# Angle and rope tables in two parts, early products of ones, and transpositions inside a unit's products

## The reference

```
w = weights[subjects]
x = x + einsum('bct,bcd->bdt', x, w)
```

```
q = rope(rmsnorm(x @ Wq.T, q_norm_w), pos)          # k likewise; v = x @ Wv.T
freqs = pos[..., None] * inv_freq                   # pos = cache_seqlens + arange(32)
rope(t) = concat([t1*cos - t2*sin, t2*cos + t1*sin])  # sin, cos of freqs
o = softmax(q @ k_all.T * SCALE, masked) @ v_all
x = x + o @ Wo.T
```

## Time and profile before

| | |
|---|---|
| median of three runs | 1021.69 us |
| lowest, highest | 1018.34, 1025.10 us |
| span of the profiled execution | 1018.6 us |
| TensorE busy | 965.9 us (95%) |
| VectorE, ScalarE, GpSimd busy | 821.1, 738.2, 536.8 us |
| first product of unit 0 | 20.44 us |
| first product of units 1, 2, 3 | 26.62, 31.51, 37.44 us |
| first product of unit 8 (chunk 1) | 64.31 us |

### The profile page before, as it was taken

The page is one execution under the profiler, slowest core; times in us unless marked ns, Lnnn a source line. Parts: engine busy times, 40 slices in busy tenths (PEclk is TensorE's granted clock), DMA queues, the critical chain, the costliest instruction groups (busy, mean ns, idle before and its releaser), DMA issues.

```text
span 1018.6 us, 24766 instructions
## 1 busy us (share of the span) xinstructions
PE 965.9 (95%) x8097; PEld 799.2 (78%) x8097; DVE 821.1 (81%) x1755; ACT 738.2 (72%) x2007; POOL 536.8 (53%) x706
## 2 busy tenths in 40 slices
PE   4889999999889988899999999999999999989998
PEld 2668888888677777787788888888888888878885
DVE  6779999999998688878877777877787787877770
ACT  4888999988784687877767676767676776767660
POOL 4445565655893057655555464455445544544440
PEclk9999999999999999999999999999999999999999
DMA  5789999989997979999999998999998999999950
GB/s 197 252 271 319 326 391 362 386 294 381 393 350 250 377 268 330 357 280 249 258 301 284 275 292 280 312 264 284 321 278 258 317 296 251 311 279 288 265 125 11
DMA packets 249903, 294.89 MB, mean 290 GB/s; under 512 B 79024, under 2 KB 206512, under 8 KB 247216
## 3 DMA queue, kind: packets, MB, share of 16 engines
q1 hardware_dynamic: 231088, 226.07, 74.6%
q0 software_dynamic: 18688, 67.25, 17.6%
HBM read 231.77 MB, written 46.27 MB: 273 GB/s over the span
## 4 chain that ended last, share of the span: by engine, by line
PE 69%; DVE 14%; issue 6%; ACT 5%; POOL 3%; DMA 1%; SPq 1%; DVEq 0%; ACTq 0%; POOLq 0%
PE ps_proj L1465 16%; PE ps_y L1465 15%; PE ps_o L1540 13%; PE ps_s L1503 7%; PE ps_t L1514 7%; PE ps_s L1507 6%; PE ps_rt L1611 2%; DVE c_stage L1361 2%; DVE rot L1333 2%; DVE probs L1209 2%; DVE stage L1347 1%; PE ps_t L1522 1%; PE ps_o L1552 1%; DVE rot L1325 1%; POOL probs L920 1%
## 5 line engine op out<-in xcount | busy, mean ns | idle before, releaser
L920 POOL TENSOR_SCALAR probs<-probs,recip 128x544 f32<-128x544 f32 (+1 forms) x256 | 162.4, 635 | 298.0 <-DVE recip L1217 290.8
L994 ACT ACTIVATE probs<-probs,neg_max 128x544 f32<-128x544 f32 x256 | 191.5, 748 | 148.9 <-DVE neg_max L1209 132.5
L1209 DVE CUSTOM_DVE_ANT_0 probs<-ps_s,mask,row_scale 128x544 f32<-128x544 f32 x256 | 200.4, 783 | 65.9 <-PE ps_s L1507 50.0
L1540 PE MATMUL ps_o<-pt,vs 128*128 128x128 f16 x3072 | 213.3, 219 | 0.5 <-DMA vs<-v_pages,v_row 0.5
L1540 PEld LDWEIGHTS ps_o<-pt,vs 128*128 128x128 f16 x3072 | 192.7, 98 | 14.9 <-DMA vs<-v_pages,v_row 0.9
L874 POOL TENSOR_TENSOR roped<-rot 128x256 f32<-128x256 f32 x160 | 144.2, 923 | 81.2 <-DVE rot L1325 78.1
L1229 DVE SCALAR_TENSOR_TENSOR pt<-ps_t,pt 128x512 f16<-128x512 f32 x190 | 130.0, 684 | 48.7 <-ACT pt L1000 42.7
L1465 PE MATMUL ps_proj<-wt_hi,x0t_hi 128*128 128x512 f32 x384 | 159.6, 416 | 7.4 <-DVE x0t_lo L1167 6.4
L1465 PE MATMUL ps_y<-wo,ot_hi 128*128 128x512 f16 x512 | 153.5, 381 | 2.6 <-DVE ot_lo L1241 2.6
L1465 PE MATMUL ps_proj<-wt_hi,x0t_lo 128*128 128x512 f32 x384 | 151.8, 395 | 0.0
L1465 PE MATMUL ps_proj<-wt_lo,x0t_hi 128*128 128x512 f32 x384 | 150.8, 393 | 0.0
(11 more groups left out here) (153 smaller groups left out, 1644.0 us busy)
## 6 DMA issues: line engine op xcount, KB each, us to landing
kt<-k_pages_t SPq DMA_DIRECT2D x512, 128.0 KB
c_nat<-in_L_cond_k_cache SPq DMA_DIRECT2D x32, 512.0 KB, 6.0
q_t<-stage SPq DMA_DIRECT2D x64, 256.0 KB, 6.8
c_nat<-in_L_cond_v_cache SPq DMA_DIRECT2D x32, 512.0 KB, 7.2
qt<-q_t SPq DMA_DIRECT2D x32, 512.0 KB
w_nat<-in_L_cond_Wq SPq DMA_DIRECT2D x8, 1024.0 KB, 8.7
k_pages_t<-c_stage SPq DMA_DIRECT2D x16, 512.0 KB, 5.8
c_nat<-in_L_cond_Wo SPq DMA_DIRECT2D x16, 512.0 KB, 7.5
```

The costliest lines, as they stand in the source:

```text
L920: pool.tensor_scalar(part, part, col(recip, i), 1.0, ALU.mult, ALU.mult).then_inc(p_norm, 1)
L994: act.activation(pr, pr, ACT.Exp, bias=col(neg_max, i), scale=-1.0, accum_out=col(row_sum, i)).then_inc(a_exp, 1)
L1209: dve.tensor_tensor_reduce(out=probs_of(i), in0=ps_s[:, score_cols(i):score_cols(i) + KEYS], in1=mask[(i // HK) % 2][:, mask_at(i):mask_at ...
L1540: ins = pe.matmul(ps_o[n % 2][:, jl * P:(jl + 1) * P], v[:, part, :], pt[pt_slot(i)][:, NCH * half + c, :], start=jl == 1 and c == 0 and k ...
```

## The change

On VectorE the angle work and the query tables are made for token tiles 0 and 1 ahead of the loop; the angles of tiles 2 to 7 follow ahead of the loop too, with tile 1's lower part amid them, and their tables inside unit 0. The work on the norm weights moves ahead of all of it. On ScalarE the sines are in two pairs accordingly, the second ahead of unit 0's squares, a sine of one column is taken at the start, and tile 0's higher part moves between the weights' higher parts. On VectorE the whole-table operations of lines 1267 to 1282, with the lower parts that followed them, are replaced by the calls shown; the seven operations on the norm weights are unchanged. On TensorE products of ones by ones, whose result nobody reads, stand at three places of the head, and in chunk 0 the transpositions of the next tile stand between the sixth and the seventh product. GpSimd issues three gathers instead of four ahead of the first weight scale. Squares of chunk 1's weights go to another scratch tile, since the angles are still in use.

```diff
+    TABLES = (slice(0, 2), slice(2, NG))
...
@@ sync
-                    sp.wait_ge(v_rope, 4)
+                    sp.wait_ge(v_rope, 6)
...
@@ gpsimd
-            for g in range(NG // 2):
+            for g in range(3):
                 gather_weights(g)
             pool.wait_ge(p_zero, 3)
             weight_scale(0)
-            for g in range(NG // 2, NG):
+            for g in range(3, NG):
                 gather_weights(g)
...
@@ scalar
-                if c >= 1:
+                if c >= 2:
                     act.wait_ge(a_wsq, HPC * c + j)
-                junk = angle[:].rearrange("p (k a) f -> p k (a f)", k=KC) if c >= 1 else w_head(wt_hi[0], j)
+                junk = angle[:].rearrange("p (k a) f -> p k (a f)", k=KC) if c >= 2 else w_head(wt_hi[c], j)
...
+            def sines(n):
+                act.wait_ge(v_ang, n + 1)
+                act.activation(sin_t[:, TABLES[n]], red_a[:, TABLES[n]], ACT.Sin)
+                act.activation(cos_t[:, TABLES[n]], red_b[:, TABLES[n]], ACT.Sin).then_inc(a_sin, 1)
+
+            act.wait_ge(p_zero, 1)
+            act.activation(norm_sums[:, 1:2], minus_one[:], ACT.Sin)
             for j in range(HPC):
                 w_squares(0, j)
-            for j in range(HPC):
-                w_high(0, j)
-            act.wait_ge(v_ang, 1)
-            act.activation(sin_t[:], red_a[:], ACT.Sin)
-            act.activation(cos_t[:], red_b[:], ACT.Sin).then_inc(a_sin, 1)
+            w_high(0, 0)
+            w_high(0, 1)
             x_high(0)
+            w_high(0, 2)
+            w_high(0, 3)
+            sines(0)
             x_squares(0)
...
                 if c == 0 and g + 1 < NG:
                     x_high(g + 1)
+                if u == 0:
+                    sines(1)
                 act.wait_ge(t_proj, u + 1)
...
@@ vector
+            def turned_angles(tiles):
+                n = tiles.stop - tiles.start
+                link(dve.tensor_tensor(angle[:, tiles], pos[:, tiles].rearrange("p (g a) -> p g a", a=1).to_broadcast((P, n, HALF_D)),
+                                       inv_freq[:].rearrange("p (a f) -> p a f", a=1).to_broadcast((P, n, HALF_D)), ALU.mult))
+                link(dve.tensor_scalar(turns[:, tiles], angle[:, tiles], 1.0 / TWO_PI, ROUND_MAGIC, ALU.mult, ALU.add))
+                link(dve.tensor_scalar(turns[:, tiles], turns[:, tiles], ROUND_MAGIC, None, ALU.subtract))
+                link(dve.scalar_tensor_tensor(red_a[:, tiles], turns[:, tiles], -C1, angle[:, tiles], ALU.mult, ALU.add))
+
+            def reduced_angles(tiles):
+                link(dve.scalar_tensor_tensor(red_b[:, tiles], turns[:, tiles], -C2, red_a[:, tiles], ALU.mult, ALU.add))
+                link(dve.scalar_tensor_tensor(red_a[:, tiles], turns[:, tiles], -C3, red_b[:, tiles], ALU.mult, ALU.add))
+                link(dve.tensor_scalar(angle[:, tiles], red_a[:, tiles], float(np.pi / 2), None, ALU.add))
+                link(dve.tensor_scalar(turns[:, tiles], angle[:, tiles], float(np.pi), TWO_PI, ALU.is_gt, ALU.mult))
+                link(dve.tensor_tensor(red_b[:, tiles], angle[:, tiles], turns[:, tiles], ALU.subtract))
+                link(dve.tensor_scalar(red_b[:, tiles], red_b[:, tiles], PI_BELOW, -PI_BELOW, ALU.min, ALU.max))
+                dve.tensor_scalar(red_a[:, tiles], red_a[:, tiles], PI_BELOW, -PI_BELOW, ALU.min, ALU.max).then_inc(v_ang, 1)
+
+            def query_tables(tiles, done):
+                dve.wait_ge(a_sin, done)
+                link(dve.tensor_scalar(nsin_t[:, tiles], sin_t[:, tiles], -1.0, None, ALU.mult))
+                for h in range(2):
+                    rope_tables("q", norm_q, h, tiles)
...
             dve.wait_ge(v_chain, chain[0])
...
-            l0_add(0)
-            w_low(0, 0)
-            w_low(0, 1)
-            w_low(0, 2)
-            x_low(0)
-            w_low(0, 3)
-            l0_add(1)
-            l0_weights(2)
             dve.wait_ge(d_norm, 16)
...
-            dve.wait_ge(a_sin, 1)
-            link(dve.tensor_scalar(nsin_t[:], sin_t[:], -1.0, None, ALU.mult))
-            for h in range(2):
-                rope_tables("q", norm_q, h)
+            turned_angles(TABLES[0])
+            l0_weights(0)
+            weight_sum(0)
+            l0_weights(1)
+            reduced_angles(TABLES[0])
+            l0_add(0)
+            w_low(0, 0)
+            w_low(0, 1)
+            x_low(0)
+            w_low(0, 2)
+            w_low(0, 3)
+            l0_add(1)
+            l0_weights(2)
+            query_tables(TABLES[0], 1)
+            turned_angles(TABLES[1])
+            x_low(1)
+            reduced_angles(TABLES[1])
 
             for u in range(NU):
                 c, g = units[u]
-                if c == 0:
-                    if g + 1 < NG:
-                        x_low(g + 1)
+                if c == 0 and 1 <= g and g + 1 < NG:
+                    x_low(g + 1)
                 if u == 0:
                     dve.wait_ge(v_rope, 2)
+                if u == TABLES[1].start:
+                    dve.wait_ge(v_rope, 4)
...
                     if u == NG * HK:
-                        dve.wait_ge(v_rope, 4)
+                        dve.wait_ge(v_rope, 6)
...
+                if u == 0:
+                    query_tables(TABLES[1], 2)
                 if c == 0 and g + 3 < NG:
                     l0_weights(g + 3)
                 if c == 0 and g + 2 < NG:
                     l0_add(g + 2)
...
@@ tensor
+            def keep_warm(times):
+                for _ in range(times):
+                    pe.matmul(ps_proj[NPJ - 1][:, 0:P], ones_p[:], ones_p[:], start=True, stop=True)
+
             pe.wait_ge(p_zero, 3)
+            pe.wait_ge(d_w[0], 16)
+            keep_warm(7)
             weight_sum(0)
             l0(0)
+            keep_warm(2)
             turn_x(0)
             l0(1)
+            keep_warm(6)
             for u in range(NU):
...
-                products(ps_proj[u % NPJ][:], pairs).then_inc(t_proj, 1)
+                middle = len(pairs) // 2
+                products(ps_proj[u % NPJ][:], pairs[:middle], last=False)
+                if c == 0 and g + 1 < NG:
+                    turn_x(g + 1)
+                products(ps_proj[u % NPJ][:], pairs[middle:], first=False).then_inc(t_proj, 1)
...
-                if c == 0 and g + 1 < NG:
-                    turn_x(g + 1)
                 if c == 0 and g + 2 < NG:
                     l0(g + 2)
```

More of the change, by code:

```diff
@@ L1131, in link, with half, rope_tables @@
                 dve.wait_ge(v_chain, chain[0])
-            def half(t, h):
+            def half(t, h, n):
                 return t[:, h * HALF_D:(h + 1) * HALF_D].rearrange("p (a f) -> p a f", a=1
-                                                                  ).to_broadcast((P, NG, HALF_D))
-            def rope_tables(kind, w, h):
+                                                                  ).to_broadcast((P, n, HALF_D))
+            def rope_tables(kind, w, h, tiles):
                 lo, hi = h * HALF_D, (h + 1) * HALF_D
-                dve.tensor_tensor(rope[kind][:, :, 0, lo:hi], cos_t[:], half(w, h), ALU.mult)
-                dve.tensor_tensor(rope[kind][:, :, 1, lo:hi], (sin_t, nsin_t)[h][:], half(w, h), ALU.mult
+                n = tiles.stop - tiles.start
+                dve.tensor_tensor(rope[kind][:, tiles, 0, lo:hi], cos_t[:, tiles], half(w, h, n), ALU.mult)
+                dve.tensor_tensor(rope[kind][:, tiles, 1, lo:hi], (sin_t, nsin_t)[h][:, tiles], half(w, h, n), ALU.mult
                                   ).then_inc(v_rope, 1)
@@ L1413, in _ @@
                     dve.wait_ge(v_scale, 1)
-                    rope_tables("k", norm_k, u - K_TABLE_AT)
+                    rope_tables("k", norm_k, u - K_TABLE_AT, slice(0, NG))
                 if u == NN:
```

## The result

The changed kernel takes 1028.55 us, median of six runs (1028.41 to 1029.39), beside 1020.91 for the kernel before in six runs. The ratio is 1.0069 with a 95% interval of 1.0046 to 1.0092: 0.7% slower. Its profiled execution has a span of 1026.7 us against 1018.6.

The account below looks back on a forecast made before the run. The start of unit 8 was taken to bound the kernel: 6.5 us late at unit 2 less 0.8 back gives 5.7, carried one for one onto 1021.69 to 1027 us; range 1018 to 1035.

Parts of the forecast that it names:

- The head: Up to unit 0's first product: 19.2 us instead of 20.44, 1.2 us earlier; range 19.2 to 21.2.
- The gap: In unit 1, tile 2's transpositions wait for the residual add, ending at 33.8; TensorE idles over 8 us.
- The clock: Array level behind unit 1's idle wait: cold at least at first, unit 2 at 38.0, 6.5 us late.
- the cold case: Remainder of unit 1 all at the lower clock level: unit 2 at 39.6, 8.1 us after its 31.51.
- Rival K: Follow-up rival: low clock after unit 1's gap is the price, 2.5 us in experiment 1; no chance given.
- Units 2 to 7: Five units at 5.6 us and a last of 4 give 32 against 32.8 before: 0.8 us back.
- the new cycle: Units of chunk 0: second half of products, squares, scale, rotation, diagonal, add, transpositions; 5.6 us against 5.4 before.
- Does it carry?: Behind unit 8: delay passed on one for one to the end, 1018.6 becoming 1024.3 us.
- (a): Faster: six-tile tables off the path in chunk 0, 9.3 us gained, so 1012; chance 0.09.
- (b): Absorbed: stages after chunk 0 give most back, 0 to 3 us late, 1023; chance 0.14.
- (c): Clearly slower: low clock level returns in each of units 2 to 7, 17 us, so 1039; chance 0.10.
- (d): Head: warm-up does nothing, unit 0 takes 4.28 us, adding under 1 us: 1028; inside the forecast's 0.67.

Follow-up runs that it names:

- experiment 1: Changed kernel with the next diagonal and residual add ahead of the wait for squares, in unit 0 alone: 1024.41 us.
- experiment 4: Changed kernel with the six-tile tables behind the residual add in unit 0: 1024.69 us.
- experiment 5: Changed kernel with the second sines behind unit 0's squares on ScalarE: 1026.20 us.
- experiment 6: Changed kernel with the second sines behind unit 0's squares and the six-tile tables behind the residual add: 1023.13 us.
- experiment 10: Kernel before with transpositions inside the products, residual add ahead of the wait for squares in all of chunk 0, and products of ones: 1017.56 us.
- experiment 11: Changed kernel with add ahead of squares wait in all of chunk 0, second sines behind unit 0's squares, six-tile tables in unit 1: 1018.78 us.
- experiment 2: Changed kernel with the transpositions back behind a unit's twelve products: 1026.41 us.
- experiment 3: Changed kernel with the next diagonal and residual add ahead of the wait for squares in all of chunk 0: 1021.22 us.
- experiment 9: Kernel before with transpositions inside the products and residual add ahead of the wait for squares in all of chunk 0, no products of ones: 1016.99 us.
- experiment 7: Kernel before with only the transpositions moved inside a unit's products: 1023.76 us.
- Experiment 8: Changed kernel without its products of ones and the wait ahead of them: 1030.01 us.

## Why the prediction was right

It gave 1027 us for a measured 1028.55, and +5.7 us for unit 8 where 7.1 were found. Against the kernel before the loss is 7.6 us (1028.55 for 1020.91). The mechanism is the one that was forecast; that the time came within 1.6 us owes something to luck: the forecast started from 1021.69, 0.8 above the median of six runs, and terms below cancel.

**The head.** First product at 19.2 forecast, 18.77 found; unit 1 at 23.7 forecast, 23.13 found. The work on the norm weights starts at 9.15 (9.4 had been taken). The head also varies with the landing of the first loads: unit 0 starts between 18.29 and 19.04 in the nine profiled executions with the changed order on VectorE, and between 19.60 and 20.44 in the four with the order of before, so the 1.7 us of the table are at the high end of what the change gives.

**The gap.** The forecast walked the two queues: last angle operation ended at 26.8 (found 26.3), sines to 27.9 (27.3), squares to 29.0 (28.3), rotation to 30.6 (29.9), tables to 32.9 (33.2), add to 33.8 (34.0). The terms were each a little long and the tables 0.9 us short; the errors cancel. Durations for 384 elements, drawn between the rows for 128 and 512, were 0.55 and 0.39 against 0.55 and 0.36 found. Experiments 1, 4, 5 and 6 each move one piece of that chain and the gap follows by the piece's own length, so the chain is shown and not only argued.

**The clock.** This is the term that was mis-sized. Unit 2 was put at 38.0, halfway between 36.6 warm and 39.6 cold, for a remainder of unit 1 that is cold "at least at first". All of it ran at the lower level: the transpositions, six products 0.43 us apart and the first layer's matmul. The record of unit 2 starts at 38.46, which looks like a hit, but its second product comes at 39.51, 7.7 us late and not 6.5. That is the cold case but for 0.4 us, since the step from the transpositions to the next product took 0.77 us and not 1.12. The rule of the Trainium skill's page "TensorE: Matmul & The Clock Gate", Part 1, that idleness brings the lower level and activity lifts it, is borne out by the 0.50 after the gap. Its case, the 39.6 of the prediction, was the better number. The clock's share in the loss can be read against the next unit of the same kernel: the transpositions and six products took 3.48 us from 34.06 and 1.88 from 41.42, and from the first layer's matmul to the second product of the next unit it was 1.97 us and 1.31, so 2.3 us of the 7.7 are the clock's and the rest is the wait. Rival K is true for that third, and only behind a gap that the queues make.

**Units 2 to 7.** Forecast: 5.6 us a unit on the new cycle, 0.8 us back in all. Found: 5.7 to 5.8 on the cycle. From the recorded start of unit 2 to that of unit 8 it is 32.9 us against 32.8 before; from second product to second product, which leaves out the long first record, 32.2 against 32.8, so 0.6 back. One round of the cycle, from the chain of waits of the changed kernel:

```profile
41.42 0.66 PE ps_tr L1510 x4
42.08 1.39 PE ps_proj L1494 x6
...
43.67 0.98 ACT squares L1070 x7
...
44.73 0.37 DVE rope_q L1348
...
45.12 1.22 DVE rot L1352
46.34 0.20 DVE w_diag L1167
46.54 0.61 DVE x L1173
...
47.20 0.66 PE ps_tr L1510 x4
```

The cycle is 0.15 us longer than worked out. The step from unit 5 to unit 6 takes 6.4 us: tile 6 is transposed at 58.63, but ScalarE takes its higher part only at 61.01, behind two pieces of chunk 1's weights and two scans. The last step, from unit 7 to unit 8, is shorter than forecast, 3.3 us for 4. So the sum reads 7.7 - 0.6 = 7.1 where the forecast had 6.5 - 0.8 = 5.7.

**Does it carry?** One for one was forecast. Unit 8 is 7.1 us later and the span 8.1 longer. The stretch behind unit 8 passes the delay on: a transposition that waits 2.35 us for GpSimd starts at 911.93 before and at 918.92 after, 7.0 us later. Behind that same wait the clock falls in the changed kernel and not in the one before (granted clock 1.00 from 912 to 916 us):

```profile
918.92 0.66 PE L1543 MATMUL ps_t<-fixed,probs 128*128 128x128 f32 x4 [2.35 <-POOL probs L921]
```

```profile
920.00:924.00 4.00, 4.00 (x31) 0.58 0.99 354
```

That stretch costs 1.7 us (4 us at 0.58 of full), which the forecast did not have: 7.1 and 1.7 make 8.8, of which 0.7 comes back elsewhere. The other kernels follow this too. In experiments 10 and 11, whose clock holds here, the span moves less than 1 us differently from unit 8 (-4.2 and -4.5, -4.0 and -4.6); in experiments 1 to 6 and 9, whose clock falls once behind unit 8, the span ends up 0.6 to 1.6 us later than unit 8 says; in experiment 7 it falls twice, the other time from 352 to 358 us, and the span is 2.6 us longer with unit 8 0.6 us earlier. Experiment 8 has no such fall, but waits 3.7 us for one result of VectorE between 345 and 365 us, where the wait before is 1.0. Most of the spread between runs of one kernel goes with the clock as well: on the third chip the kernel before took 1016.7 to 1019.8 us in the six runs with a mean granted clock of 1.000 and 1027.1 in the one with 0.991. Why the clock falls behind one wait and holds behind the same wait in another execution stays open. The rows for 70 to 80 us did not show that TensorE has no gap later; it has such waits, but they moved with the rest.

**The rivals.** (a), tables off the path, did not occur, but its mechanism is what experiments 9 and 10 bring about by leaving them undivided: 4.2 us ahead at unit 8, of the 9.3 it would have given. (b) is refuted by the carry. (c), the low level returning in every unit, is not seen: the waits in units 2 to 6 were 0.6 to 1.3 us and the clock stayed at 1.00 (stretch, PE busy with count, PEclk, DMA share, GB/s):

```profile
40.00:71.00 31.00, 25.13 (x116) 1.00 0.55 177
```

(d) did not occur: the first layer's two products took 2.04 us from 12.35 and 1.02 from 15.77, and the array was at its higher level from the first product of unit 0 on.

## What to carry to other kernels

Before an operation is moved into another's pipeline, find what it waits for and where that stands in its own engine's queue: the transposition moved half a unit ahead, the add that feeds it did not, and the tables put ahead of the add were needed by no one before unit 2. A piece of work taken off the head must land somewhere; put it behind what other engines wait for, not ahead. An engine's long idle time at one instruction (4.8 us at the sines) doesn't tell what moving that instruction is worth (2.2 us), since the next engine on the path may be busy all the while.

## What the hardware showed

The six-tile tables took 3.2 us and not 2.3, because the first two of the four multiplications were slow. VectorE's timeline, and GpSimd's at the same time:

```profile
30.31 0.96 DVE L1151 TENSOR_TENSOR rope_q<-cos_t,norms 128x384 f32<-128x384 f32 x1
31.19 1.07 DVE L1152 TENSOR_TENSOR rope_q<-sin_t,norms 128x384 f32<-128x384 f32 x1
32.19 0.54 DVE L1151 TENSOR_TENSOR rope_q<-cos_t,norms 128x384 f32<-128x384 f32 x1
32.66 0.55 DVE L1152 TENSOR_TENSOR rope_q<-turns,norms 128x384 f32<-128x384 f32 x1
```

```profile
30.09 1.76 POOL L875 TENSOR_TENSOR roped<-rot 128x256 f32<-128x256 f32 x2 [0.25 <-DVE rot L1352]
```

While GpSimd adds the halves of unit 0 (30.09 to 31.85), VectorE's multiplication of two SBUF operands of 384 elements takes 0.96 and 1.07 us; once GpSimd is done, 0.54 and 0.55. The same is seen in the other kernels with six-tile tables. In experiments 4 and 6 only the first multiplication overlaps GpSimd's adds, and only that one is slow (0.97 and 0.96 us; the second, slow above, takes 0.54 and 0.55). GpSimd's two adds took 1.76 us beside two slow ones, 1.57 beside one, and 1.41 to 1.45 beside other work. The Trainium skill's "GPSIMD Engine Reference", section 1, says that GpSimd's SBUF interfaces are shared with VectorE and contended by VectorE instructions with two SBUF inputs; this trace agrees. The price here is 0.9 us for VectorE over two multiplications and 0.3 us for GpSimd over two adds.
